# A two-layer adaLN feed-forward and mixture-of-experts block on one core: the dense rows become routed rows, padding lanes are skipped by an index bound, and z is stored in column pieces

## The reference, cut to what matters

```python
x = x + _L0_ffn_ref(_L0_cond_ref(...), w1, w2, w3)
z = _L1_cond_ref(x, cond[:, None, :])        # causal depthwise conv, 16 taps, 512 channels
logits = einsum('bsd,de->bse', z, Wr)        # 8 experts
w, sel = top_k(logits, 2);  w = softmax(w)
for e in range(8):                           # gate is w at the two chosen experts, else 0
    out = out + gate[..., e:e+1] * (einsum('bsd,df->bsf', z, We[e]) + be[e])
x = x + out
```

## Time and profile before

| | |
|---|---|
| median of three runs | 838.45 us |
| the profiled execution | 835.71 us |
| its span | 833.9 us |
| TensorE busy | 740.0 us (89%) |
| VectorE, ScalarE, GpSimd busy | 542.5, 435.2, 490.4 us |
| mean clock granted to TensorE | 0.958 of full |

### The profile page before, as it was taken

The page is one execution under the profiler, slowest core; times in us unless marked ns, Lnnn a source line. Parts: engine busy times, 40 slices in busy tenths (PEclk is TensorE's granted clock), DMA queues, the critical chain, the costliest instruction groups (busy, mean ns, idle before and its releaser), DMA issues.

```text
span 833.9 us, 13284 instructions
## 1 busy us (share of the span) xinstructions
PE 740.0 (89%) x3835; PEld 489.1 (59%) x3874; DVE 542.5 (65%) x784; ACT 435.2 (52%) x716; POOL 490.4 (59%) x756
## 2 busy tenths in 40 slices
PE   1744689999999999999999799997879999999994
PEld 0111245555555555655555489985668888888883
DVE  2467989888888888758885335684553665444442
ACT  2055466778777787567776423571432343333331
POOL 1036888777877777747762320012553888888873
PEclk9986899999999999989999998998799999999997
DMA  9985136566677877537655466868965899999985
GB/s 359 387 308 171 32 77 111 117 145 140 146 150 148 165 138 149 127 80 165 140 105 114 86 125 46 278 243 286 293 109 95 150 163 168 165 167 165 167 151 76
DMA packets 224504, 133.55 MB, mean 160 GB/s; under 512 B 181090, under 2 KB 185186, under 8 KB 223282
## 3 DMA queue, kind: packets, MB, share of 16 engines
q1 hardware_dynamic: 206770, 92.17, 45.2%
q0 software_dynamic: 15456, 36.26, 23.8%
q10 hardware_dynamic: 2208, 4.28, 1.6%
HBM read 74.18 MB, written 37.52 MB: 134 GB/s over the span
## 4 chain that ended last, share of the span: by engine, by line
PE 73%; DMA 9%; SPq 7%; DVE 4%; issue 3%; POOL 2%; ACT 2%; POOLq 0%; DVEq 0%; ACTq 0%
PE PS L1847 20%; PE PS L1654 12%; PE PS L1666 12%; PE PS L1677 12%; PE PS L1731 6%; PE PS L1698 3%; PE PS L1828 3%; SPq L436 2%; DMA z_scratch<-ZS 2%; SPq L521 2%; DMA WRT<-in_Wr 2%; PE PS L1707 2%; PE PS L1689 1%; PE PS L1819 1%; DMA QyT<-Qy 1%
## 5 line engine op out<-in xcount | busy, mean ns | idle before, releaser
L1847 PE MATMUL PS<-W,ZH 128*128 x552 | 179.9, 407 | 8.8 <-DVE W L1377 8.8
L1654 PE MATMUL PS<-W,QyT 128*128 128x512 bf16 x499 | 124.8, 391 | 27.3 <-DMA QyT<-Qy 16.5
L897 POOL DMA_INDIRECT out_x<-YS,IDS x69 | 109.4, 1585 | 58.2 <-ACT YS L1125 32.0
L1125 ACT ACTIVATE YS<-YS,SG 128x512 f32<-128x512 f32 x69 | 50.0, 724 | 152.8 <-DVE YS L1574 120.8
L1666 PE MATMUL PS<-W,QyT 128*128 128x512 bf16 x500 | 121.5, 382 | 0.6
L1847 PEld LDWEIGHTS PS<-W,ZH 128*128 128x128 f32 x552 | 100.5, 192 | 28.0 <-issue 10.0
L1677 PE MATMUL PS<-W,QT 128*128 128x512 bf16 x498 | 114.7, 381 | 0.9 <-issue 0.2
L888 POOL DMA_INDIRECT ZR<-z_scratch,IDG x69 | 69.8, 1011 | 70.0 <-DVE IDG L1498 32.3
L1847 PE MATMUL PS<-W,ZL 128*128 x276 | 109.8, 398 | 0.0
L1549 DVE TENSOR_TENSOR ZL<-PS,ZH 128x512 fp32r<-128x512 f32 x69 | 47.7, 692 | 91.1 <-ACT ZH L1111 91.1
L958 ACT ACTIVATE SG<-PS,sm 128x1024 f32<-128x1024 f32 x64 | 71.3, 1114 | 60.0 <-PE PS L1654 60.0
(11 more groups left out here) (267 smaller groups left out, 1171.2 us busy)
## 6 DMA issues: line engine op xcount, KB each, us to landing
X<-in_x SPq DMA_DIRECT2D x32, 256.0 KB, 10.0
out_x<-X SPq DMA_DIRECT2D x32, 256.0 KB, 2.5
WRAW<-in_We SPq DMA_DIRECT2D x8, 1024.0 KB, 10.4
ST<-out_x SPq DMA_DIRECT2D x28, 256.0 KB, 3.6
XR<-in_x SPq DMA_DIRECT2D x20, 256.0 KB, 3.5
z_scratch<-ZS SPq DMA_DIRECT2D x1, 4112.0 KB, 16.0
z_scratch<-ZS ACTq DMA_DIRECT2D x1, 4112.0 KB, 17.3
stage<-in_w1T SPq DMA_DIRECT2D x4, 1024.0 KB, 7.8
```

The lines of the kernel that those rows point to most:

```text
L897: pool.indirect_dma_start(x1_d, bass.IndirectOffsetOnAxis(IDS[:, m:m + 1].bitcast(U32), 0), YS[m % UN][:], None, compute_op=ALU.add).then_ ...
L1654: i = nc.tensor.matmul(GP[:, a, :], QyT[t][:, k, :], W12[:, k, o:o + CH], start=(k == 0), stop=(k == KD - 1))
L1847: x = nc.tensor.matmul(bank[i], zz[i % 2][:, k, :], W2[:, bass.ds(q, 1), part, k, :].rearrange("p o d -> p (o d)"), start=(k == 0 and n == ...
```

## The change

- All 32 token columns are routed. `turn_zd`, `dense`, `acc_expert`, `acc_bias`, the load and the store of `ACC` and the lists for the dense column are gone. `MT` goes from 69 to 71.
- A padding lane gets the output row `TOK + 1` and more, and the scatter has a bound (`bounds_check=TOK - 1`, `oob_is_err=False`) above which a lane is skipped.
- `evict` writes the bank's 32 channels side by side, so that z's columns are in the order of the convolution. The experts' rows are loaded in the same order, in four DMAs of 256 KB for each expert.
- z is stored in four column pieces for each half (20, 20, 16 and 8 of the 64 channel steps: rows of 640, 640, 512 and 264 B), each as soon as its groups are evicted. SyncE stores the four of half 0 and the first two of half 1, ScalarE the last two of half 1. SyncE's experts 0 and 1 and the first bias load change places around them.
- Some tables move in SBUF; semaphore values follow.

```diff
-    MT = NK - 2 + E - 1
+    MT = NK + E - 1
-    ND = OB - 1
+    SPLIT = [0, 5, 10, 14, 16]
...
+        def store_z(queue, h, part):
+            first, end = (GI * NJ * SPLIT[part + i] for i in range(2))
+            if part + 2 == len(SPLIT):
+                end = ZW
+            queue.dma_start(bass.AP(z_d.tensor, h * BH * S * ZW + first, [[OB * ZW, P], [ZW, OB], [1, end - first]]),
+                            ZS[h][:, :, first:end].bitcast(I32)).then_inc(z_out[h], 16)
...
@@ block.sync
-            sp.dma_start(ACC[:], bass.AP(out.tensor, ND * D, [[OB * D, CB], [S * D, BH], [1, D]])).then_inc(acc_in, 16)
...
-                sp.dma_start(WRAW[e][:], We[e].rearrange("(k p) f -> p k f", p=P)).then_inc(w_in[1][e % (E // 2)], 16)
+                for k in range(KD):
+                    sp.dma_start(WRAW[e][:, k, :], bass.AP(We.tensor, (e * D + P // NJ * k) * D, [[D, P // NJ], [NI * D, NJ], [1, D]])) \
+                        .then_inc(w_in[1][e % (E // 2)], 16)
...
-            sp.wait_ge(z_done, NG)
-            sp.wait_ge(gates_in, 1)
-            sp.dma_start(z_rows(0), ZS[0][:, :, 0:ZW].bitcast(I32)).then_inc(z_out, 16)
+            for part in range(4):
+                sp.wait_ge(z_done, SPLIT[part + 1])
+                if part == 3:
+                    sp.wait_ge(gates_in, 1)
+                store_z(sp, 0, part)
+            sp.wait_ge(z_out[0], 64)
+            load_expert(1)
+            load_bias(0, LATE)
+            sp.sem_inc(z_out[1], 1)
+            sp.wait_ge(z_done, NG + SPLIT[1])
+            store_z(sp, 1, 0)
             sp.wait_ge(conv_done, NG + 7)
             load_expert(0)
-            sp.wait_ge(z_out, 16)
-            sp.wait_ge(zdt_done, 1)
-            load_expert(1)
-            load_bias(0, LATE)
+            sp.wait_ge(z_done, NG + SPLIT[2])
+            store_z(sp, 1, 1)
             sp.wait_ge(conv_done, NG + 11)
             load_expert(2)
...
-            sp.wait_ge(acc_done, 2 * E)
-            sp.dma_start(bass.AP(out.tensor, ND * D, [[OB * D, CB], [S * D, BH], [1, D]]), ACC[:]).then_inc(out_done, 16)
-            sp.wait_ge(out_done, 16)
...
@@ block.gpsimd
                 if m == LATE:
-                    pool.wait_ge(z_out, 32)
+                    pool.wait_ge(z_out[1], 65)
...
                 pool.indirect_dma_start(x1_d, bass.IndirectOffsetOnAxis(IDS[:, m:m + 1].bitcast(U32), 0), YS[m % UN][:], None,
-                                        compute_op=ALU.add).then_inc(y_out[m % UN], 16)
+                                        bounds_check=TOK - 1, oob_is_err=False, compute_op=ALU.add).then_inc(y_out[m % UN], 16)
...
@@ block.scalar
-                nc.scalar.copy(ZS[h][:, :, 0:D].rearrange("p s (j i) -> p s j i", j=NJ)[:, :, :, i:i + GI],
-                               bank[r % 4].rearrange("p (i j o) -> p o j i", i=GI, j=NJ)[:, ::-1]).then_inc(z_done, 1)
+                nc.scalar.copy(ZS[h][:, :, NJ * i:NJ * i + NJ * GI],
+                               bank[r % 4].rearrange("p (c o) -> p o c", o=OB)[:, ::-1]).then_inc(z_done, 1)
...
                 if r in (27, 29):
                     high((r - 27) // 2)
-            act.wait_ge(z_out, 16)
+                if r == NG + SPLIT[3] - 1:
+                    act.wait_ge(z_done, r + 1)
+                    store_z(nc.scalar, 1, 2)
             act.wait_ge(gates_in, 2)
             act.wait_ge(z_done, 2 * NG)
-            nc.scalar.dma_start(z_rows(1), ZS[1][:, :, 0:ZW].bitcast(I32)).then_inc(z_out, 16)
+            store_z(nc.scalar, 1, 3)
...
@@ block.tensor, in slot(m, i, q)
-                if m < LATE:
-                    dense(m + 1)
                 if m + 1 == LATE:
-                    dense(E // 2 - 1)
                     turn_r(m + 1, (i + 1) % UN)
-                if 0 <= m - E < E // 2:
-                    dense(m - E + E // 2)
```

More of the change, by code:

```diff
@@ L226, in adaln_ffn_moe @@
         b2 = (E + 1) * (NT + 1) + 7
[L227 to L230, removed]
+        WAITS = place("WAITS", b, [P, E, NT], I32)
+        HITS = place("HITS", b + NR, [P, E, NT])
+        assert b % 8 == 0 and b2 % 8 == 0 and b + 2 * NR <= a_bd + 3 * GI * 2 * P
         a = a_h + OB * ZP
@@ L238, in adaln_ffn_moe @@
         a += CC * MT
-        ZDH, ZDL = (place(n, a + D * i, [P, KD, P], F32R) for i, n in enumerate(("ZDH", "ZDL")))
-        a += 2 * D
+        UPTO = place("UPTO", a, [P, E + 1, NT + 1])
+        a += b2
         TEXP, TPLC, IDG, IDS = (place(n, a + MW * i, [1 if i < 2 else P, MT], I32) for i, n in
@@ L286, in adaln_ffn_moe @@
         a += 3 * NK
-        ACC = place("ACC", a, [P, D])
-        a += D
         assert a <= a_s + 8 * D + 5 * (D // 2) + 2 * D + FF // 2
@@ L308, in adaln_ffn_moe @@
         st_in, xw_copied, xw_v = [sem(f"st_in{i}") for i in range(2)], sem("xw_copied"), sem("xw_v")
-        z_out, z_free = sem("z_out"), sem("z_free")
+        z_out, z_free = [sem(f"z_out{h}") for h in range(2)], sem("z_free")
         ext_in = sem("ext_in")
@@ L641, in _ @@
             sp.wait_ge(slots_done, 1)
-            halves = [sp.value_load(FLAG[0:1, m:m + 1], min_val=16, max_val=32) for m in range(LATE)]
+            halves = [sp.value_load(FLAG[0:1, m:m + 1], min_val=1, max_val=65) for m in range(LATE)]
             for half in halves:
-                sp.wait_ge(z_out, half)
+                sp.wait_ge(z_out[1], half)
                 sp.sem_inc(z_free, 1)
@@ L1064, in numbers @@
                     act.wait_ge(tab_done, q - 1)
-                for c in range(listed(q)):
+                for c in range(CC):
                     i = nc.scalar.activation(BOH[q % 2][:, c, 0, :], BOX[q % 2][:, c, :], ACT.Copy, scale=float(c + 1 + CC * (q // 2)))
-                    if c % 4 == 3 or c == listed(q) - 1:
+                    if c % 4 == 3:
                         i.then_inc(num_done, 1)
             def high(e):
-                act.wait_ge(w_in[1][e % (E // 2)], 16 * (2 + 2 * e // E))
+                act.wait_ge(w_in[1][e % (E // 2)], 16 + 16 * KD * (1 + 2 * e // E))
                 nc.scalar.copy(W2[:, where[e], 0], WRAW[e][:]).then_inc(wh_done, 1)
@@ L1801, in _ @@
                     prefix()
-                if r == 17:
-                    turn_zd()
                 if r in (22, 24, 26, 28):
                     table((r - 22) // 2)
-            def dense(n, first=0, last=KD):
-                e = n
-                pe.wait_ge(w_low, n + 1)
-                if n == 0:
-                    pe.wait_ge(zdl_done, 1)
-                if n == 2:
-                    pe.wait_ge(first_done, 2)
-                if n >= 2:
-                    pe.wait_ge(acc_done, n - 1)
-                for k in range(first, last):
-                    for j, (zz, part) in enumerate(((ZDH, 0), (ZDH, 1), (ZDL, 0))):
-                        x = nc.tensor.matmul(bank[6 + n % 2], zz[:, k, :], W2[:, where[e], part, k, :],
-                                             start=(k == 0 and j == 0), stop=(k == KD - 1 and j == 2))
-                if last == KD:
-                    x.then_inc(dense_done, 1)
             def turn_r(m, i):
@@ L1832, in _ @@
             turn_r(0, 0)
-            dense(0)
             def slot(m, i, q):
```

72 lines of the change are left out of this document (9 added, 63 removed).

## The result

| | before | after |
|---|---|---|
| median | 838.5 us (8 runs) | 842.41 us (840.34 to 846.15, 8 runs) |
| the profiled execution | 835.71 us | 843.15 us |
| its span | 833.9 us | 841.1 us |
| mean clock granted to TensorE | 0.958 | 0.944 |

The account below looks back on a forecast made before the run. TensorE was taken to bound the steady slots, with GpSimd 0.01 us behind; -11.2 + 12.8 - 8.4 - 10.0 + 1.2 = -15.6 us from the 838.45 us median gave 822.8 us, range 813 to 836 us.

Parts of the forecast that it names:

- z in pieces: Stores of z before slot 2's gather: early pieces fit where DMA engines ran at 0.41, z lands earlier; -10.0 us.
- Rival 2: Stores of z: short runs take longer, z lands no earlier, the 10 us saving shrinks to nothing, 832.8 us; chance 0.09.
- The dense matmuls: Eight matmul groups go: experts 4 to 7 behind slots 8 to 11 save 11.2 us, experts 0 to 3 nothing.
- Two more slots: Routed slots: the last slot with tokens becomes 68 instead of 64, four slots at 3.19 us, +12.8 us.
- The end: After the last useful slot's matmuls start their end: 15.5 us follow instead of 23.9, so -8.4 us.
- low end: Bottom of the forecast range: padding scatters that move nothing may land up to 3 us sooner, not counted in the sum.
- Rival 3: Padding scatters: skipped lanes are moved like others, the sum stays, only 3 us lost; no chance of its own.
- 0.2 to finish: Last part of the kernel's end: 0.2 us from the last padding scatter's landing to the end of the span.
- The bound on the scatter: Scatter issue on GpSimd: the option costs 0.03 us, the cycle becomes 3.21, slots 8 to 68 pay +1.2 us.
- Rival 1: Scatter issue in slots 8 to 68: GpSimd becomes the bound, 827 to 838 us (chance 0.13) or up to 900 (0.16).

## Why the prediction was wrong

**The step that failed is "z in pieces"**, -10.0 us in the sum. It measured +12.3 us at slot 2's gather (573.73 to 586.03) and +13.1 at its transposes (581.37 to 594.46). It went wrong in three places.

*The price of a piece.* I priced the early pieces as 2.6 MB with room to move in, and what was left as bytes at 246 GB/s. The packets of the DMA queue say what was to be counted. Before, 522 to 532 us, nothing but half 0 in whole rows:

```profile
q1 hardware_dynamic: 1364, 2.80, 82.5%
```

After, 521 to 532 us, nothing but pieces:

```profile
q1 hardware_dynamic: 3866, 2.33, 115.9%
```

Columns are packets, MB and share of 16 engines. A packet of a whole row, 2053 B by these figures, takes 16 x 10 us x 0.825 / 1364 = 97 ns of an engine, one of a piece, 603 B, 16 x 11 us x 1.159 / 3866 = 53 ns. Less than a third of the bytes takes over half the time. A half in four pieces then takes about 2.2 times as much of the engines' time; lone, 31 us against 15.6.

*The bound from the nearest row.* "2048 runs of 256 B took 5.0 us" was a load of aligned rows of the output. A store of as many runs of 264 B at 2056 B distance took 7.6 us alone. I hadn't asked how the rows lie. In the kernel the last piece took 18.38 us, with other pieces and loads under way beside it: from 556 to 577 us the DMA engines were at 1.09 to 1.12 of their share.

*What stands behind a piece.* I read the stretch at 0.41 as room for pieces and took SyncE's order as harmless ("only loads that now come earlier"). The loads came later. Half 0's pieces landed at 542.8, expert 0 was loaded behind them and behind the first piece of half 1, and ScalarE waited 11.76 us for it in front of the evictions that make the last pieces. So the forecast's issue times (554.4 and 556.1) became 564.57 and 567.39. How much of the loss this wait makes by itself is open, since versions that take it away without touching the stores weren't tried with unaligned pieces; with aligned ones its removal gave nothing, and with all pieces at the end there was no such wait and the loss was as large.

**Rival 2 had the mechanism** ("the same bytes take longer in short runs") but ended at "the saving shrinks to nothing". A store that takes twice as long has no reason to stop at zero. The packets of before gave 97 ns for 2053 B; nothing there showed how much of the 97 ns shrinks with the bytes, so 0.09 was too small a chance.

**The dense matmuls**: -11.2 as forecast. No dense line is in the trace, and experts 0 to 3 indeed cost nothing: TensorE stood idle 10.20 us before slot 2's transposes.

**Two more slots**: slot 68 is the last with tokens. Its matmuls start at 822.20; at 3.19 a slot, slot 8 started at 630.8 (the chain of waits has 630.58), before at 617.2 (slot 13's 644.37 less five slots and four dense groups). That is +13.6, within a microsecond of what the gather and transposes were late, so slots 2 to 7 passed the delay on unchanged.

**The end**: 16.1 us against 15.5 forecast and 23.9 before, which is near by luck, as two terms were off and cancel. One is the landing of a padding scatter, costed at 4.8 us as before. The view of DMA issues has, with the same bound and no lane above it (the kernel before, from 821 us), and in the changed kernel (from 831 us):

```profile
out_x<-YS,IDS POOLq DMA_INDIRECT x4, 4.8
...
out_x<-YS,IDS POOLq DMA_INDIRECT x2, 2.7
```

A scatter of skipped lanes lands 2.1 us sooner. The prediction had kept that for its low end. Rival 3, by which padding lanes are moved like others, fell with it. The scatter of slot 68 landed sooner as well (3.65 for 4.91). The other term is "0.2 to finish": the last scatter has landed at 837.2, and the span goes on for another 3.9 us with no DMA of the kernel under way. In the kernel before, the store of ACC stood in that place with 3.3 us, so taking it away gave nothing; what fills the 3.9 us the trace doesn't show.

**The bound on the scatter**: forecast +1.2, measured 0 (0.9999 [0.9984, 1.0014] by itself). Rival 1, with 0.29 in chances, fell: 1.589 us a scatter with the bound, 1.59 without. The rule that gave it its tail, about 12 cycles for a data-dependent branch (the Trainium skill, GPSIMD Engine Reference, section 3.1), doesn't carry over to this instruction: by it the scatter would have taken an estimated 1.3 us longer, and it took no longer.

The profiled sum is +13.6 for z, -11.2, +12.8 and -7.8 for the end: +7.4, against +7.4 between the two profiled executions. The forecast without its z term is -5.6, or -6.8 with the bound at nothing; the versions with both halves in whole rows gave -3.2 to -7.6 us by their ratios. With aligned rows the changed kernel reaches -11.4, and 827.3 us lies in the range, but that doesn't bear the z term out: slot 2's gather starts there at 571.79, 1.9 us earlier than before, where 10.0 was forecast. That term wasn't reached by any version.

## What to carry to other kernels

Price a store by its number of runs and the time that a run of its length holds a DMA engine, both read from the packets of a stretch in which nothing else moves, and only then by bytes. Cutting rows to start earlier can pay only while their extra time stays hidden, and no run here shows that it paid: two pieces came out as whole rows did. Look at the distance of the rows too: a few bytes of something else at the end of each row can cost more than the cut itself, and padding to 32 B is a one-line edit. A term that was right in its sum can still be two wrong ones: compare each part of it with the trace. And a rival that takes a saving away should be carried through zero when its mechanism has no stop there.

## What the runs showed of the hardware

- Stores to HBM of 2048 rows of 2056 B took 16.2 us with rows 2056 B apart and 12.8 with 2560 B (12.9 for rows of 2080 B at 2080); runs of 640 B took 8.06 at 2056 and 6.06 at 2080. Multiples of 32 B were enough: with rows 2304 B apart, where the 512 B run starts at a multiple of 256 B, it took 5.29 us, against 5.46 at 2080 B. The Trainium skill (DMA: Bandwidth & Descriptors, "How a descriptor splits into AXI transactions") tells of descriptors that start off a multiple of 256 B and says that what is fetched before their start costs beats. In these stores the side that is written was changed, and nearly all of the difference was between on and off a multiple of 32 B.
- With rows 2056 B apart 2048 runs of 128 B took 6.8 us, hardly less than the 7.9 of 512 B.
- Issuing can hold an engine while earlier DMAs are under way: four pieces that were all ready took ScalarE 18.74 us to issue (0.57 the quickest, 6.35 the slowest), where one whole half took 0.57. (SyncE's 20.36 us for half 0's four have some 2 us of waiting for evictions in them.) An engine that issues pieces between its other work can be held by them, as ScalarE was for 6.50 us.
- A bounded scatter of 128 rows costs GpSimd what an unbounded one does, 1.59 us. With all lanes above the bound it landed in 2.7 us, with all below it in 4.8.
